# Two mixture-of-experts stages of a decoder kernel: groups of one and three batches, rows sent tile by tile, hidden units on partitions

## The reference

```
stage 11:  xn = layernorm(x)                     # 2048 tokens x 256
  gout = xn @ Wg.T                               # 8 scores per token
  topv, topi = top_k(gout, 2);  w = softmax(topv)
  g = xn @ W1[e].T + b1[e];  v = xn @ W2[e].T + b2[e]   # 512 units each
  out = sum over the 2 chosen e of w_e * ((silu(g) * v) @ W3[e].T + b3[e])
  x = x + out
stage 8:   the same form, with sigmoid scores, one up projection of 512
           units, relu(.)**2 in place of silu(g)*v, and no biases
```

## Time and profile before

| | |
|---|---|
| median of 3 runs | 4053.84 us (4048.78 to 4055.82) |
| the profiled execution | 4056.98 us, span 4055.3 us |
| busy share of the span | PE 87%, PEld 53%, DVE 54%, ACT 34%, POOL 34% |
| mean granted TensorE clock | 0.923 of full speed |
| stage 8 | from 2745.9 to about 3051 us |
| stage 11 | from 3670.1 us to the end |

### The profile page before, as it was taken

The page is one execution under the profiler, slowest core; times in us unless marked ns, Lnnn a source line. Parts: engine busy times, 40 slices in busy tenths (PEclk is TensorE's granted clock), DMA queues, the critical chain, the costliest instruction groups (busy, mean ns, idle before and its releaser), DMA issues. The chain is left out here.

```text
span 4055.3 us, 51579 instructions
## 1 busy us (share of the span) xinstructions
PE 3533.7 (87%) x17642; PEld 2130.7 (53%) x17642; DVE 2170.5 (54%) x5215; ACT 1392.9 (34%) x3007; POOL 1365.9 (34%) x1976
## 2 busy tenths in 40 slices
PE   7998888899999786888799999995977789985996
PEld 5675674455555574444444545454653444544653
DVE  5374354554646486664465757563234366663443
ACT  3243103443434462333344444431322044441221
POOL 2142342332423263233445454533112244443011
PEclk9999879999999897998899999996988799996998
DMA  2001000000000000000100000003210000005121
GB/s 97 1 1 60 14 6 40 1 1 1 1 0 1 12 1 23 1 1 1 47 1 1 1 1 1 1 1 145 76 62 19 28 1 1 1 1 228 49 63 62
DMA packets 49121, 106.61 MB, mean 26 GB/s; under 512 B 6564, under 2 KB 38692, under 8 KB 46692
## 3 DMA queue, kind: packets, MB, share of 16 engines
q1 hardware_dynamic: 42724, 86.53, 5.9%
q0 software_dynamic: 6144, 16.79, 1.3%
HBM read 74.72 MB, written 28.57 MB: 25 GB/s over the span
## 5 line engine op out<-in xcount | busy, mean ns | idle before, releaser
L2628 POOL TENSOR_SCALAR probs<-probs,inv_sum 128x512 f32<-128x512 f32 x640 | 434.7, 692 | 962.3 <-DVE inv_sum L2749 962.1
L2586 ACT ACTIVATE probs<-psum_banks,neg_max 128x576 f32<-128x576 f32 x640 | 468.1, 736 | 710.2 <-DVE neg_max L2828 710.2
L2828 DVE TENSOR_REDUCE neg_max<-psum_banks 128x1 f32<-128x576 f32 x640 | 454.7, 752 | 193.0 <-PE psum_banks L2461 186.4
L2461 PE MATMUL psum_banks<-keys_T,queries_T 64*128 64x288 f32 x2560 | 406.0, 436 | 40.1 <-ACT probs L2586 28.0
L2758 DVE COPY probs_T<-psum_banks 128x512 f32<-128x512 f32 x640 | 408.8, 680 | 20.0 <-PE psum_banks L2390 20.0
L2461 PEld LDWEIGHTS psum_banks<-keys_T,queries_T 64*128 64x128 f32 x2560 | 225.0, 189 | 266.2 <-ACT probs L2586 160.4
L2390 PE MATMUL psum_banks<-ident,probs 128*128 128x128 f32 x2560 | 351.0, 280 | 3.2 <-POOL probs L2628 2.3
L2390 PEld LDWEIGHTS psum_banks<-ident,probs 128*128 128x128 f32 x2560 | 275.6, 141 | 129.8 <-POOL probs L2628 73.3
L2420 PE MATMUL psum_banks<-probs_T,values 128*64 128x512 f32 x1280 | 307.4, 604 | 2.2 <-issue 2.2
L4329 PE MATMUL psum_banks<-w_L_experts_up,sorted_T 128*128 x552 | 258.1, 604 | 0.3 <-issue 0.3
L4265 POOL DMA_INDIRECT normed<-expert_outputs,row_index x64 | 65.1, 1017 | 443.8 <-DMA expert_outputs<-expert_rows 425.5
(11 more groups left out here) (526 smaller groups left out, 6196.2 us busy)
## 6 DMA issues: line engine op xcount, KB each, us to landing
expert_outputs<-expert_rows SPq DMA_DIRECT2D x92, 128.0 KB, 1.7
group_normed_T<-sorted_rows SPq DMA_DIRECT2D x20, 512.0 KB, 4.1
w_L_experts_down<-in_L_experts_down SPq DMA_DIRECT2D x2, 4096.0 KB, 23.0
row_vectors<-in_rows SPq DMA_DIRECT2D x1, 5120.0 KB
sorted_rows<-zero_rows SPq DMA_DIRECT2D x4, 1024.0 KB, 9.1
w_L_xattn_Wkv<-in_L_xattn_Wkv SPq DMA_DIRECT2D x2, 2048.0 KB, 8.4
w_L_experts_up<-in_L_experts_up SPq DMA_DIRECT2D x1, 4096.0 KB, 12.2
x_res<-in_x SPq DMA_DIRECT2D x4, 512.0 KB, 7.0
```

The costliest lines, as they stand in the source:

```text
L2461: last = pe.matmul(k.ps[:, 2 * h + a, 0:HALF], qT[r, b % 2, j, t * P:(t + 1) * P], kT[r, j, k0:k0 + HALF], start=True, stop=True)
L2586: act.activation(prob[:, g % PB, h * w:(h + 1) * w].rearrange("p (a n) -> p a n", a=2), k.ps[:, 2 * h:2 * h + 2, 0:HALF], ACT.Exp, bias=nm ...
L2628: pool.tensor_scalar(w, w, inv[:, g % 4, h:h + 1], 1.0, ALU.mult, ALU.mult).then_inc(shared, 1)
L2828: dve.tensor_reduce(nmax[:, g % 4, h:h + 1], k.ps[:, 2 * h:2 * h + 2, 0:HALF], AX.XY, ALU.max, negate=True).then_inc(maxed, 1)
```

## The change

**Groups and preparation.** Group 0 is now 4 token tiles (one batch) with 15 sorted tiles, group 1 is 12 token tiles with 31; the sum stays 46. VectorE normalises group 0, ScalarE group 1 (`Identity` with scale and bias). TensorE transposes and routes in four pieces of 4 token tiles through one transposed buffer of 4 tiles; it no longer waits for `placed` of group 1 before the loop. Group 1's ranking is put into the loop: in step 1 TensorE does `rank(1)` and VectorE `put(1)` and `weigh(1)`.

**Rows sent tile by tile.** Every row in the sorted array gets a 257th number, the DRAM row in which its result belongs (2 x token + slot + 1; 0 in an unused row). The arrays of zeroed rows are now two sets, one per stage. For slot 1 ScalarE makes a second copy of group 0's rows (`again`) and GpSimd adds one to the number of group 1's rows after slot 0 has landed. In the loop VectorE takes the numbers out of each loaded chunk (`take_ids`; unused rows get a spare row), and GpSimd scatters each finished tile with one indirect DMA (`scatter_rows`) in place of SP's contiguous store. A batch's results then lie contiguously, and SP fetches them with one plain DMA per batch (`fetch`: 1024 KB): batch 0 beside the loop, three after it. Chunks are 3 tiles.

**Hidden units on partitions.** The up projection is turned round: the weights are stationary and the sorted rows move, so the hidden units come out on partitions and `turn_hidden` and `move_hidden` go.
**The end.** Stage 11 stores the output batch by batch as it is combined; the block after it is gone.

```diff
-GROUPS = 2
-GT = NT // GROUPS
-CHUNK = 4
+GROUP_TILES = (4, 12)
+GROUP_SORTED = tuple((2 * n * P + E * (P - 1)) // P for n in GROUP_TILES)
+CHUNK = 3
+ROW = D + 1
...
                 def project_up(n):
...
-                    at[n] = pe.value_load(up_at[0:1, g, i:i + 1], min_val=0, max_val=(E - 1) * STEP)
+                    pe.wait_ge(weights_copied, n + 1)
                     for part in range(UP // 512):
-                        for c in range(KC):
-                            last = pe.matmul(ps[:, 2 * (n % 2) + part, :], xsT[:, n % RX, c, :],
-                                             w_up[:, c, part * 512:part * 512 + (E - 1) * STEP + 512][
-                                                 :, bass.ds(at[n], 512)], start=c == 0, stop=c == KC - 1)
+                        for f in range(4):
+                            for c in range(KC):
+                                last = pe.matmul(ps[:, 2 * (n % 2) + part, f * P:(f + 1) * P],
+                                                 wt[:, n % 2, c, part * 512 + f * P:part * 512 + (f + 1) * P],
+                                                 xsT[:, n % RX, c, :], start=c == 0, stop=c == KC - 1)
                         last.then_inc(up, 1)
...
-                for g in range(GROUPS):
-                    normed_turned(g)
-                    route(g)
-                    rank(g)
-                pe.wait_ge(placed, GROUPS)
-                pe.wait_ge(weights_in, 16 * (2 + len(k.stage_rows)))
+                piece_turned(0)
+                route(0)
+                rank(0)
+                piece_turned(1)
+                for p in range(1, PIECES):
+                    if p + 1 < PIECES:
+                        piece_turned(p + 1)
+                    route(p)
...
-                for n in range(NTILES + 2):
+                for n in range(NTILES + 1):
                     if n < NTILES:
                         project_up(n)
-                    if n >= 2:
-                        project_down(n - 2)
-                    if 1 <= n <= NTILES:
-                        turn_hidden(n - 1)
+                    if n == 1:
+                        rank(1)
+                    if n >= 1:
+                        project_down(n - 1)
                     if n + 2 < NTILES:
                         turn_rows(n + 2)
...
+                def copy_weights(n):
...
+                    if n >= 2:
+                        act.wait_ge(up, UP // 512 * (n - 1))
+                    at = act.value_load(up_at[0:1, n:n + 1], min_val=0, max_val=(E - 1) * STEP)
+                    act.copy(wt[:, n % 2, :, :], w_up[:, :, 0:(E - 1) * STEP + UP][:, :, bass.ds(at, UP)]).then_inc(
+                        weights_copied, 1)
...
+                def scatter_rows(n):
+                    pool.wait_ge(ids_taken, chunk_of[n][0] + 1)
+                    pool.wait_ge(rows_made, n + 1)
+                    pool.indirect_dma_start(
+                        outputs[:, :], bass.IndirectOffsetOnAxis(out_at[:, n:n + 1], 0), y[:, n % RY, :], None,
+                        bounds_check=2 * NT * P + NTILES * P, oob_is_err=False).then_inc(stored[n % RY], 16)
...
+                for t in range(GROUP_FIRST[1], NT):
+                    scatter(t, rows[:, t, :], 0, scattered_1)
+                    if t % 3 == 0:
+                        scatter_rows(done)
+                        done += 1
+                pool.wait_ge(scattered_1, later_scattered)
```

More of the change, by code:

```diff
@@ L4256, in _ @@
[L4256 to L4268 removed]
+                    pool.tensor_tensor(rs[:, 1, n], rs[:, 0, n], k.half[:, 0:GROUP_TILES[g]], ALU.pow).then_inc(rstd, 1)
@@ L4304, in rank @@
+                    for t in range(n):
+                        last = pe.matmul(ranks[g][:, t + 1:n + 1, :], k.ones[:, :],
+                                         mask[g][:, t:t + 1, :].to_broadcast([P, n - t, E]), start=False,
+                                         stop=t == n - 1)
                     last.then_inc(ranked, 1)
@@ L4509, in _ @@
[L4509 to L4519 removed]
+                    o.mark(dve.memset(mask[g][:, GROUP_TILES[g], :], 0.0))
@@ L4575, in _ @@
+                for t in range(TT, NT):
+                    combine(t, t - TT)
                 dve.wait_ge(combined, NT)
```

593 lines of the change are left out of this document (345 added, 248 removed).

## The result

The changed kernel takes **3984.45 us** (median of 4 runs, 3976.31 to 3991.49), the kernel before 4051.31 beside it: ratio 0.9834, 95% interval 0.9811 to 0.9856. Forecast were 3981, in a range of 3953 to 4015. The profiled execution took 3976.31 us, its span 3974.6, 80.7 less than the span before.

What follows compares the result with a forecast made beforehand. TensorE was taken to set both loops, with nothing hiding the work outside them. Terms of -35.5 us in stage 8 and -38.5 in stage 11 sum to -74, giving a forecast of 3981 us, range 3953 to 4015.

Steps and rivals of the forecast that it cites:

- the sum: Total of the forecast terms for stages 8 and 11: -35.5 and -38.5 us, together -74 us.
- The step: One tile's pass through either loop: fewer transposes, turned up projection; over 46 steps -17 us in stage 8, -14.5 in stage 11.
- The sixteen records: 128-column TensorE records with their own weights, 0.111 us each, taken as the cost of the turned up projection's records.
- 0.162 us for a record of two passes: Up projection, rival that weight loads bind: at this record cost the time would be 4093 us; chance 0.05.
- Preparation of stage 8: Stage start to first up projection: smaller group 0 brings it to 39.5 us, a gain of 23.5 us.
- Preparation of stage 11: Stage start to first up projection: at 43 us, a gain of 20 us, with SP's row load queued behind the weights.
- the last scatter lands slower: Stage 11 preparation: group 0's last scatter was taken to land 2.8 us after its end on GpSimd.
- Ranking in the loop: Group 1's ranking, moved into the loop, stops TensorE: +8 us in stage 8, +5.5 in stage 11.
- Group 1's data late: Stage 8's TensorE waits at tile 15: +3 us, stage 11 0; rival, late in both stages, 4001 us, chance 0.08.
- Tails: After TensorE's end: last combine at 22.5 us, -4.5 us in stage 8; with output pieces, -8 us in stage 11.
- Holds: Rivals on stalls in both loops: more, twice 31 us lost, 4012 us, chance 0.18; fewer, 3960 us, chance 0.17.
- Its signs of being wrong: Both loops: steps over 6 us, TensorE waiting for `tile_weights`, or holds in the steady part would refute the forecast.

Runs made afterwards that it cites:

- e3: Changed kernel with stage 8 alone given back the old up projection (rows stationary, hidden rows transposed, no weight copies): 3989.08 us, ratio 0.9858.
- e10: The kernel before, unchanged, run again on the third chip for its trace: 4019.80 us in a single run.
- e9: The changed kernel, unchanged, run again on the third chip: 3952.13 us, ratio 0.9824 to the kernel before.
- e1: Changed kernel with stage 11's `w_down` load issued after the two loads of sorted rows instead of ahead of them: 3976.81 us, ratio 0.9824.
- e8: Changed kernel with `w_down` later, tile 0's weights copied first, stage 11's group 1 exponential behind the first copies, `weigh(1)` in step 3: 3946.91 us, ratio 0.9815.
- e7: Changed kernel with a GpSimd pause after each of group 1's 24 scatters in both stages: 4020.31 us, ratio 0.9992.
- e12: Changed kernel with stage 11's output stored in one DMA after the last combine instead of four pieces: 3954.60 us, ratio 0.9834.
- the first group's traces: Traces of four follow-up variants of the changed kernel run on one chip, with the kernel before beside them at 4048.61 us.
- e6: Changed kernel with each tile of stage 11's result rows scattered four times, three to memory nobody reads: 3984.52 us, ratio 0.9907.

## Why the prediction was right

The forecast of 3981 met 3984. In the traces of record stage 8 gave 12 us more than the sum has, stages 0 to 7 took 5 back, and stage 11 hit its sum with a preparation 7 us worse and the rest 7 us better. So the mechanism of the step was right, and that the total came within 4 us is in part luck: the total is better than its parts. By its steps:

- **The step: right to the hundredth.** 3.73 and 5.52 us, 0.111 per record. The sixteen records of the earlier trace rows held for 2208. The Trainium skill's 81 ns per matmul ("TensorE: Matmul & The Clock Gate", section Back-to-back issue gap), read as 0.162 us for a record of two passes, is not what this loop shows; that section names no data type, and the doubling was the prediction's own reading. e3 turned the step back to 4.10.
- **Preparation of stage 8: right.** First up at 37.5 for 39.5. But about 5 us of the gain of 25.5 is a hold of the kernel before: the wait of 4.08 us of the earlier trace rows, which the prediction took for a part of the path, is not there in e10.
- **Preparation of stage 11: wrong by 7.3 us**, the largest miss. The step that failed is "the last scatter lands slower (2.8 us from its end at 3720.19 to 3722.95)". That row was taken beside weights that had all but arrived. Here GpSimd is done earlier, at 3656.2, with 4 MB of `w_down` still to come, and every small packet of a scatter waits its turn behind a large one: 13.6 us, and 13.5 again in e9's trace. The prediction had seen the queue on SP's side (the load stands behind the weights) and not that the scatters meet the same engines. e1 moved the weights and took 9.4 us of it back.
- **Ranking in the loop: +5.8 and +5.1** for +8 and +5.5, the two stops of each stage over the step (6.64 and 6.66 in stage 8, 8.43 and 7.76 in stage 11). TensorE's 2.9 us are real work; the rest goes if `weigh(1)` comes later (e8: second stop 0.6).
- **Group 1's data late: 0** in the execution of record, where two holds had already delayed TensorE; 1.1 us on the chip without holds (one step of 4.80), for +3. The order on GpSimd that sets it was not priced: with 24 pauses it costs 42.6 us (e7).
- **Tails: 2.1 and 3.9 us better than forecast.** Three fetches of 1024 KB with combines of 0.92 instead of 1.03, and output pieces, which e12 prices at 3.3 us of the 12.0 gained.
- **Holds: neither doubled nor halved in the loops.** 26.5 us for 32. "All four in the loops came while GpSimd had indirect DMAs in a row" was true, and is true of every bunch in the first group's traces, but such a stream alone does not make one: e6 has 196 in a row and none, and e9 and e10 have the same streams as the traces of record and none. By medians their price is nearly the same for both kernels, 29.6 us before (4051.31 to 4021.69) and 32.3 after (3984.45 to 3952.13), so it nearly cancels in the ratio (0.9834 and 0.9824). In the two traces of record it does not: stages 8 and 11 are 43.3 us longer than in e10 before and 25.2 longer than in e9 after. Some 18 us of the 80.7 between these two traces are holds and what follows them, 8.4 of them in stage 8, where they are most of the 12 us over its sum.
- **Its signs of being wrong were drawn too wide.** TensorE did wait for `tile_weights`, 4.9 us, at the two starts and in no later step, and holds did come in the loops, as they had before. Neither says that the sum is wrong.

On the chip without holds the parts come out cleaner (e10's trace against e9's): preparations -19.9 and -9.2, loops -11.3 and -7.7, tails and output -7.8 and -11.7, together -67.6 us for a sum of -74. Stage 8 gives 39.0 for 35.5 and stage 11 28.6 for 38.5, and the largest part of what is missing is stage 11's preparation. The medians there differ by 69.6; the spans of the two traces differ by 59.1 only, as stages 0 to 7 took 10.3 us longer in e9's.

What in a chip, beside it or in the recording makes the updates late was not found; e6 and e7 were meant to tell, and ran where there was nothing to tell.

## What to carry to other kernels

When a stage loads weights in bulk while GpSimd scatters rows that the stage waits for, order the bulk by its due time: issue behind the small transfers what is not needed first. A DMA's landing time from one trace holds only with the same traffic beside it. When an engine's copy runs beside a bound engine, double it once: that tells how much room there is better than adding up busy times.

## What the hardware showed that was not expected

- **Late semaphore updates.** In some groups of runs bunches of semaphore updates, TensorE's above all but VectorE's too, arrived 3 to 9 us late, two or three times per stage, always beside GpSimd's indirect DMAs in a row, and the two traces of record lack some 1,000 and 1,500 of 18,000 update records; otherwise TensorE's come within 0.02 us. The page shows it only as "remote" idle time. The kernel before took 4051 and 4048.61 us in the groups of runs with such holds and 4023.00 and 4021.69 in those without.
- **Two queues in turn, by packets.** 120 packets of 3.78 MB against 117 of 0.29 MB in the same 10 us: a scatter beside bulk loads gets a half of the turns and a fourteenth of the bytes.
- **The same matrix work costs twice ahead of a loop.** 24 ranking records took 5.17 us in stage 8's preparation, at a granted clock of 0.50, and 2.76 inside the loops of stage 8 and stage 11, at 1.00: here, work that TensorE must do anyway was cheaper behind its own busy stretch than in front of it.
